# Re-ordering the preparation of a fused four-layer kernel: adapter tables laid out by the host, the convolution kernel's factors in another order, and its product behind two weight blocks

## The reference

```
x = x + mask * (causal_conv(mask*x, K) + D*mask*x)           # K[h,l] = 2 Re sum_n Cs[h,n] exp(dtA[h,n]*l), 64 states
x = x + einsum('bct,bcd->bdt', x, mix_weights[cond])          # 16 x 64 x 64
x = x + x @ base_weight.T + bias + (x @ A[ad].T) @ B[ad].T    # 32 adapters of rank 16
x = x + x @ W.T + 0.5 * (x @ lora_A[lab]) @ lora_B.T          # 5 labelers of rank 32
```

## Time and profile before

| | us |
|---|---|
| runs: median (lowest to highest) of 3 | 1478.62 (1477.57 to 1480.40) |
| the profiled execution, its own time | 1480.16 |
| its span in the profile | 1478.4 |
| preparation, to TensorE's first convolution matmul | 200.07 |
| convolution, to its last matmul | 571.4 |
| busy in the span: PE / VectorE / ScalarE / POOL | 1434.4 / 1140.7 / 612.5 / 119.0 |
| mean granted TensorE clock | 0.994 |

### The profile page before, as it was taken

How to read it: one execution, slowest core, us unless ns; L and a number is a source line. 1 busy time by engine, 2 the same in 40 slices (tenths; PEclk the granted TensorE clock), 3 DMA queues, 4 the chain that set the end, 5 groups by cost and what they waited for, 6 DMA issues and landing times.

```text
span 1478.4 us, 31603 instructions
## 1 busy us (share of the span) xinstructions
PE 1434.4 (97%) x9344; PEld 1330.9 (90%) x9344; DVE 1140.7 (77%) x2298; ACT 612.5 (41%) x1217; POOL 119.0 (8%) x188
## 2 busy tenths in 40 slices
PE   6989989999999997999999999999999999999998
PEld 5877879999999996889999999999999999999998
DVE  7974488888888885777777777777777777777775
ACT  3331256566666653334334334334334334334332
POOL 3460210000000000000000000000000000000000
PEclk9999999999999998999999999999999999999999
DMA  8034168888888887554655655655655655655652
GB/s 311 20 136 114 26 206 285 274 275 272 272 276 274 274 274 193 174 152 149 206 146 164 201 148 169 197 146 168 197 149 167 199 147 166 200 149 163 200 155 79
DMA packets 121523, 276.15 MB, mean 187 GB/s; under 512 B 23913, under 2 KB 64365, under 8 KB 118833
## 3 DMA queue, kind: packets, MB, share of 16 engines
q1 hardware_dynamic: 111308, 241.28, 54.1%
q10 hardware_dynamic: 10182, 34.46, 5.9%
HBM read 200.72 MB, written 74.95 MB: 186 GB/s over the span
## 4 chain that ended last, share of the span: by engine, by line
PE 86%; DVE 7%; DMA 3%; POOL 1%; issue 1%; ACT 1%; SPq 0%; DVEq 0%; ACTq 0%; POOLq 0%
PE ps L1601 18%; PE ps L1594 15%; PE ps L1232 13%; PE ps L1593 11%; PE ps L1574 8%; PE ps L1243 6%; PE ps L1134 4%; PE ps L1610 4%; PE ps L1223 3%; PE ps L1235 2%; DMA out<-y_out 1%; PE ps L1585 1%; DVE p L808 1%; DVE b3t L904 1%; DMA b_d<-b_last 1%
## 5 line engine op out<-in xcount | busy, mean ns | idle before, releaser
L1593 PE MATMUL ps<-weights,xa 128*128 128x256 f32 x1152 | 321.8, 282 | 2.3 <-ACT y_out L1384 1.6
L1594 PE MATMUL ps<-weights,xa 128*128 128x352 f32 x1152 | 322.7, 322 | 0.0
L1601 PE MATMUL ps<-weights,xs 128*128 128x512 f32 x1152 | 291.2, 401 | 0.0
L1601 PEld LDWEIGHTS ps<-weights,xs 128*128 128x128 f32 x1152 | 207.0, 189 | 40.4
L1232 PE MATMUL ps<-toep,ut 128*128 128x512 f32 (+2 forms) x1152 | 226.8, 342 | 0.0
L1593 PEld LDWEIGHTS ps<-weights,xa 128*128 128x128 f32 x1152 | 217.4, 189 | 4.9 <-issue 3.4
L1594 PEld LDWEIGHTS ps<-weights,xa 128*128 128x128 f32 x1152 | 216.2, 188 | 1.4
L1232 PEld LDWEIGHTS ps<-toep,ut 128*128 128x128 f32 x1152 | 194.3, 189 | 16.6
L1360 ACT ACTIVATE a<-ps 128x512 f32<-128x512 f32 x128 | 76.7, 599 | 288.1 <-PE ps L1574 272.6
L1574 PE MATMUL ps<-m_gath,x_in 128*128 128x128 f32 x1024 | 137.9, 279 | 10.3 <-DVE x_in L1459 10.3
L1574 PEld LDWEIGHTS ps<-m_gath,x_in 128*128 128x128 f32 x1024 | 129.6, 195 | 13.3 <-DVE x_in L1459 10.8
(11 more groups left out here) (223 smaller groups left out, 2262.6 us busy)
## 6 DMA issues: line engine op xcount, KB each, us to landing
lags<-kern_d SPq DMA_DIRECT2D x64, 512.0 KB, 5.0
xt<-in_xt SPq DMA_DIRECT2D x64, 512.0 KB, 5.7
x_d<-yo SPq DMA_DIRECT2D x64, 512.0 KB, 2.9
x_nat<-in_x SPq DMA_DIRECT2D x64, 512.0 KB, 3.8
x_in<-x_d SPq DMA_DIRECT2D x64, 512.0 KB, 5.6
out<-y_out ACTq DMA_DIRECT2D x62, 512.0 KB, 6.1
tab<-a_d SPq DMA_DIRECT2D x128, 128.0 KB, 2.1
stack<-b_d SPq DMA_DIRECT2D x126, 128.0 KB, 4.0
```

The costliest lines, as they stand in the source:

```text
L1593: mm(acc[:, left, 0:HALF], x_part, w[:, 0:HALF], start=start, stop=end, skip_group_check=True)
L1594: ins = mm(acc[:, right, 0:HALF + KR], x_part, w[:, HALF:WIDE], start=start, stop=end, skip_group_check=True)
L1601: ins = mm(acc[:, bank], operand[:, a, i, :], plain(i, b, m), start=opens and i == a == b == 0, stop=i == K4 - 1 and a == 1, skip_group_ch ...
```

## The change

The host lays out two inputs: the adapters' A as the table that a2_d was (so a2_d is the input itself), and the labelers' B transposed. Their transposes, copies, load and store go; the labelers' B is loaded straight into b3t after row has read it, and scaled there. The factors are formed with other instructions: POOL keeps the two first tables and the second table of turns, and VectorE does all products, the sum and the second decay table (twelve passes over 128x2048 on VectorE instead of ten, three on POOL instead of six). VectorE also makes the low part of b2_2. k0 and k1 come after d1 and d5. PSUM areas are dealt out anew; b2_3 is no longer in an area that the convolution uses. lower_low(0) moves ahead of six of the bias products, sums_low(0) and the halves of d1 and d5 ahead of the kernel's copy, and sums_low(3), which gets an argument that picks single subtractions, into channels 1 to 4. The mix load moves up on SP, behind the constants' stores; its additions on POOL come between the staging of d5 and the identities of d3 and d7. The late loads of d3 and d7 wait for `factors`. The lags of channel 1 get a buffer of their own, lags_first, which lies over yo0, so ScalarE waits before its first write to yo0.

```diff
     row_d = nc.dram_tensor("row_d", [2, T], F32).ap()
-    a2_d = nc.dram_tensor("a2_d", [A2N, P, K8 * R2], F32).ap()
...
-        ("c", 1), ("row", 0), ("b3", 3), ("k0", 2), ("k1", 1), ("la0", 0), ("la1", 3), ("la2", 2), ("la3", 1),
-        ("d1", 0), ("d5", 3), ("d2", 2), ("d6", 0), ("d3", 1), ("d7", 2), ("b2_3", 3)]
+        ("c", 1), ("row", 0), ("d1", 3), ("d5", 2), ("k0", 1), ("k1", 0),
+        ("d2", 3), ("d6", 2), ("d3", 1), ("d7", 2), ("b2_3", 0)]
     J = {name: j for j, (name, _) in enumerate(ORDER)}
...
+
+    def lags_of(k, u):
+
+        return lags_first if isinstance(k, int) and k == 0 and u == 1 else lags[u % BUFS]

...
             sp.dma_start(b2raw3[:], lora2_b[:, :, 3 * P:AR]).then_inc(in_b2_3, 16)
-            sp.dma_start(b3_raw[:], lora3_b).then_inc(in_b3, 16)

             sp.wait_ge(job_free, freed("a3b"))
             sp.dma_start(a3_d.rearrange("l p n -> p l n"), lora3_out[:].rearrange("p l c r -> p l (c r)")).then_inc(a3_stored, 16)
-            sp.wait_ge(job_done, done("a3b"))
-            sp.dma_start(lora_a_raw[:], lora2_a.rearrange("(c a) r t -> (a r) c t", c=AR // P)).then_inc(in_la, 16)
             for m in range(3):
                 sp.wait_ge(job_free, freed(f"b2_{m}"))
                 sp.dma_start(b2_rows[m * P:(m + 1) * P], f(b2_out[:])).then_inc(b2_stored, 16)
+            sp.wait_ge(job_done, done("row"))
...
             sp.dma_start(c_d[AR:AR + 1], c_row[:]).then_inc(c_stored, 16)
+            sp.wait_ge(factors, 1)
+            for v in range(2):
+                load_p2(p2_late[v], (3, 7)[v], in_late[v])
             sp.wait_ge(split_const, 4)
             sp.dma_start(row_d.unsqueeze(0), f(b2_out[0:1])).then_inc(const_stored, 16)
             sp.dma_start(b3_d, f(b2_out[B3_ROWS])).then_inc(const_stored, 16)
+            for half in range(2):
+                sp.dma_start(mix[C * half:C * half + C], mix_w.rearrange("s c d -> c s d")).then_inc(in_mix, 16)
             sp.wait_ge(kern_ready, 1)
             sp.dma_start(kern_d[:, 0:T].rearrange("h (q r) -> q h r", q=G), kern[:]).then_inc(kern_stored, 16)
-            sp.wait_ge(job_done, done("k1"))
-            for v in range(2):
-                load_p2(p2_late[v], (3, 7)[v], in_late[v])
-            sp.wait_ge(job_free, freed("la3"))
...
-            for half in range(2):
-                sp.dma_start(mix[C * half:C * half + C], mix_w.rearrange("s c d -> c s d")).then_inc(in_mix, 16)
             sp.wait_ge(p3_part, 1)
+            load_lags(0, 1)
             load_x(0, 1)
             sp.wait_ge(job_done, JOBS)
-            load_lags(0, 1)
             load_lags(0, 2)
...
             tt(fac_t[:], across(0), steps_of(0), ALU.mult).then_inc(fac_decay, 1)
-            pool.wait_ge(fac_exp, 1)
-            pool.wait_ge(fac_sin, 1)
-            link(tt(fac_u[:], fac_u[:], fac_t[:], ALU.mult))
-            tt(fac_u[:], fac_u[:], across(2), ALU.mult).then_inc(fac_sum, 1)
-            stage_low(4)
             pool.wait_ge(fac_arg, 2)
             tt(fac_v[:], across(1), steps_of(1), ALU.mult).then_inc(fac_turns, 1)
-            pool.wait_ge(fac_mid, 1)
-            tt(fac_t[:], across(0), steps_of(1), ALU.mult).then_inc(fac_decay, 1)
+            pool.wait_ge(staged_lo, 5)
             for n in range(5, len(STAGED)):
                 stage_low(n)
                 if n == 6:
+                    pool.wait_ge(in_mix, 32)
+                    for half in range(2):
+                        rows = slice(C * half, C * half + C)
+                        link(tt(mix[rows], mix[rows], ident[rows, C * half:C * half + C].unsqueeze(1).to_broadcast([C, S1, C]),
+                                ALU.add))
                     for v in range(2):
                         p2_identity(p2_late[v], (3, 7)[v], in_late[v])
-
-            pool.wait_ge(in_mix, 32)
-            for half in range(2):
-                rows = slice(C * half, C * half + C)
-                link(tt(mix[rows], mix[rows], ident[rows, C * half:C * half + C].unsqueeze(1).to_broadcast([C, S1, C]), ALU.add))
...
             act.wait_ge(part_ready, 1)
-            act.wait_ge(bias_ready, 1)
             lower_high(0)
             upper_high(0)
             act.wait_ge(fac_decay, 1)
             nc.scalar.activation(fac_t[:], fac_t[:], ACT.Exp).then_inc(fac_exp, 1)
+            stage_high(4)
             act.wait_ge(fac_arg, 1)
             trig(fac_u[:], -TWO_PI, phase[:, 3:4])
             act.wait_ge(fac_arg, 2)
             trig(fac_w[:], -TWO_PI, phase[:, 4:5])
             act.wait_ge(a3_stored, 16)
             b2_high(0, b2_out)
-            stage_high(4)
+            stage_high(5)
+            act.wait_ge(b2_stored, 16)
+            b2_high(1, b2_out)
             act.wait_ge(fac_decay, 2)
             nc.scalar.activation(fac_t[:], fac_t[:], ACT.Exp).then_inc(fac_exp, 1)
             act.wait_ge(fac_arg, 3)
             trig(fac_w[:], -TWO_PI, phase[:, 5:6])
-            for m in (1, 2):
-                act.wait_ge(job_done, done(f"b2_{m}"))
-                act.wait_ge(b2_stored, 16 * m)
-                b2_high(m, b2_out)
-                stage_high(m + 4)
+            act.wait_ge(b2_stored, 32)
+            b2_high(2, b2_out)
+            stage_high(6)

...
                 ready(act, x1_stored[u % 2], count_in(k, u, 2))
+                if isinstance(k, int) and k == u == 0:
+                    act.wait_ge(toep_lo, 2)
+                    act.wait_ge(tri_ready, 2)
                 copy(yo[u % 2][:, 0:HB], ps[2 + u % 2][:, 0:HB], ACT.Copy).then_inc(y_front, 1)
...

-            dve.wait_ge(w3_ready, K8)
-            bias_products(0, 2)
-            dve.wait_ge(job_done, done("par"))
-            t = target("par")
-            nc.vector.tensor_copy(part[:], t[:, HB:HB + 4 * C].rearrange("p (j h) -> p j h", j=4)).then_inc(part_ready, 1)
-            bias_products(2, K8)
...
                 tt(to[:, 1], target(f"b2_{m}"), f(to[:, 0]), ALU.subtract).then_inc(job_free, 1)

+            dve.wait_ge(w3_ready, K8)
+            bias_products(0, 2)
+            dve.wait_ge(job_done, done("par"))
+            t = target("par")
+            nc.vector.tensor_copy(part[:], t[:, HB:HB + 4 * C].rearrange("p (j h) -> p j h", j=4)).then_inc(part_ready, 1)
             dve.wait_ge(kern_stored, 16)
             lower_low(0)
+            bias_products(2, K8)
...
+                return grid[:, j, :].unsqueeze(1).to_broadcast([P, C, G])
+
+            dve.wait_ge(staged_hi, 5)
+            dve.wait_ge(staged_lo, 4)
+            tt(staged[0][:, 1], STAGED[4][1], f(staged[0][:, 0]), ALU.subtract).then_inc(staged_lo, 1)
...

+            dve.wait_ge(fac_sin, 1)
+            link(tt(fac_u[:], fac_u[:], across(2), ALU.mult))
+            dve.wait_ge(fac_sin, 2)
+            link(tt(fac_w[:], fac_w[:], across(3), ALU.mult))
+            b2_low(0, b2_out)
+            link(tt(fac_u[:], fac_u[:], fac_w[:], ALU.add))
             dve.wait_ge(fac_exp, 1)
-            dve.wait_ge(fac_sin, 2)
-            tt(fac_w[:], fac_w[:], fac_t[:], ALU.mult).then_inc(fac_mid, 1)
-            dve.wait_ge(fac_mid, 1)
-            link(tt(fac_w[:], fac_w[:], across(3), ALU.mult))
+            tt(fac_u[:], fac_u[:], fac_t[:], ALU.mult).then_inc(fac_sum, 1)
             dve.wait_ge(fac_sum, 1)
-            link(tt(fac_u[:], fac_u[:], fac_w[:], ALU.add))
-            b2_low(0, b2_out)
+            tt(fac_t[:], across(0), steps_of(1), ALU.mult).then_inc(fac_decay, 1)
             dve.wait_ge(fac_turns, 2)
             reduced(fac_w[:], fac_v[:], 2)
+            b2_low(1, b2_out)
             dve.wait_ge(fac_exp, 2)
             dve.wait_ge(fac_sin, 3)
             tt(fac_v[:], fac_w[:], fac_t[:], ALU.mult).then_inc(factors, 1)
-            b2_low(1, b2_out)
             b2_low(2, b2_out)
...
-            dve.wait_ge(job_done, done("b3"))
-            ts(b3t[B3_ROWS], target("b3")[0:R3, :], 0.5, None, ALU.mult).then_inc(job_free, 1)
-            dve.wait_ge(job_free, freed("b3"))
+            dve.wait_ge(in_b3, 16)
+            ts(b3t[B3_ROWS], b3t[B3_ROWS], 0.5, None, ALU.mult).then_inc(b3_scaled, 1)
+            dve.wait_ge(b3_scaled, 1)
+            dve.wait_ge(job_free, freed("row"))
             dve.wait_ge(b2_stored, 48)
...

+            sums_low(0)
+            dve.wait_ge(staged_lo, 7)
+            dve.wait_ge(c_stored, 32)
+            lower_low(1)
+            upper_low(1)
...
             tt(kern[:, :, G - 1], kern[:, :, G - 1], dcol[:], ALU.add).then_inc(kern_ready, 1)
-            for i in range(4):
-                dve.wait_ge(job_done, done(f"la{i}"))
-                nc.vector.tensor_copy(lora2_out[:, :, 2 * i:2 * i + 2, :].rearrange("p a c r -> p c a r"),
-                                      target(f"la{i}").rearrange("p (c a r) -> p c a r", c=2, a=A2N)).then_inc(job_free, 1)
-
-            dve.wait_ge(staged_lo, 7)
-            dve.wait_ge(c_stored, 32)
-            lower_low(1)
-            upper_low(1)
-            sums_low(0)
             sums_low(1)
             dve.wait_ge(staged_lo, 9)
```

(28 more changed lines are left out.)

39 lines of the change are left out of this document (19 added, 20 removed).

## The result

| | before | after |
|---|---|---|
| median of the comparison's runs (4 each) | 1479.07 | 1456.82 |
| ratio | | 0.9847 [0.9835, 0.9858] |
| the profiled execution, own time / span | 1480.16 / 1478.4 | 1456.56 / 1454.8 |
| first matmul of b2_0 / c / b2_3 | 56.6 / 95.8 / 186.5 | 52.8 / 85.6 / 168.2 |
| first matmul of convolution 0 / 3 | 200.1 / 220.2 | 179.0 / 198.1 |

The change saves 22.3 us. I had forecast 18.2 and a time of 1460.4: the direction was right, the size 4 us short, and the time lies at the lower edge of the range given. 22.1 us of it are there when convolution 3 begins (220.2-198.1), and nothing is lost in the long stages behind it. The two profiled executions are 23.6 us apart; 1.2 of the rest lies at the passage from the convolution to the products, which varies from execution to execution.

A forecast was written before the change was run, and what follows sets the result against it. TensorE, busy 97% of the span, was taken as the bound, so only removed matmuls and stops could gain. 1.6+6.3+1.0+7.3+2.5-0.5 = 18.2 us off the median 1478.62 gave 1460.4 us, range 1456.8 to 1465.2.

The forecast's parts named there:

- step 1: Ahead of b2_0: d0's low half moves before six bias products, so b2_0 no longer waits; gain 1.6 us.
- step 2: Ahead of b2_2: its low half moves to VectorE, removing the 4.76 us wait and 1.52 of slow clock; gain 6.3 us.
- step 8: End of preparation: mix's additions and VectorE's last four sums leave, removing the wait before convolution 0; gain 2.5 us.
- step 9: Before convolution 3: last store taken as 7.0 us, wait 2.8 us where it was 2.3; gives back 0.5 us.
- Steps 3 and 4: Between c and d1: b3's eight transposes go, gain 1.0 us, and the lora_A jobs go, gain 7.3 us.
- Step 5: k moves behind d1 and d5: factors ready near 97, k asked for at 122.6; cost nothing.
- Step 6: Ahead of d2: mix's load, additions and identities move before POOL's staging of d2; cost 0 to 0.4, taken as 0.
- C: At d2: it waits behind mix on POOL, the constants' split being no earlier; saving 12 to 16, about 1464.6; chance 0.10.
- D: Same place as C, mix landing after 136 us: slower than before, 1481 or more; chance 0.02.
- E: At b2_2: still waits because VectorE's low half comes after 81; 6.3 us missing, 1466.7; chance 0.03.
- rival B: Channel 3 eats nothing: store takes 5.2 us; saving 20.0 to 21.0, 1458.6 to 1457.6; chance 0.12.
- rival A: Channel 3 eats more: store takes 8.06 us and the clock falls; saving 15.6, 1463.0; chance 0.20.

The follow-up runs named there:

- again: Each kernel run a second time without edit: before 1480.45 us, changed 1459.07 us (ratio 0.9854 to the kernel before).
- third: Each kernel run a third time without edit: before 1481.13 us, changed 1457.51 us (ratio 0.9844 to the kernel before).
- bias_first: Changed kernel with the six bias products ahead of d0's low half again: 1461.26 us, ratio 0.9875 to the kernel before.
- low_half_pool: Changed kernel with b2_2's low half back on POOL, behind its tables: 1462.95 us, ratio 0.9880 to the kernel before.
- Old_factors: Changed kernel with the factors' products and the order of b2_low(1) and b2_high(1) as before: 1466.08 us, ratio 0.9911 to the kernel before.
- the tables alone: Kernel before with only both host layouts and without jobs b3 and la0 to la3: 1468.90 us, ratio 0.9920 to the kernel before.
- k_early: Changed kernel with k0, k1 and VectorE's copy of them ahead of d1 and d5 again: 1457.74 us, ratio 0.9852 to the kernel before.
- sums_back: Changed kernel with sums_low(3) whole in front of the convolution again: 1457.55 us, ratio 0.9850 to the kernel before.
- mix_late: Changed kernel with the mix load and its additions where they were before: 1458.74 us, ratio 0.9856 to the kernel before.
- no_last_store: Changed kernel without b2_last's store and channel 3's wait for it, adapters 24 to 31 wrong: 1456.64 us, ratio 0.9833 to the kernel before.

## Why the prediction came out short

The three executions of each kernel (the first profile, again, third) give each stage's mean; the table sets it against the steps' sums.

| stage | before | after | gain | forecast |
|---|---|---|---|---|
| to b2_0 (step 1) | 56.0 | 53.3 | 2.7 | 1.6 |
| b2_0 to c (step 2) | 38.8 | 32.8 | 6.0 | 6.3 |
| c to b2_3 (steps 3 to 6) | 92.2 | 82.6 | 9.6 | 8.3 |
| b2_3 to convolution 0 (step 8) | 13.5 | 10.9 | 2.6 | 2.5 |
| convolution 0 to 3 (step 9) | 20.3 | 19.1 | 1.2 | -0.5 |
| sum | 220.8 | 198.7 | 22.1 | 18.2 |

- **Step 1** had the right mechanism (bias_first puts the stop back) and was mis-sized by 1.1. I read 1.58 us off an execution in which TensorE was late by its own chance. b2_0's start before was set by VectorE (55.7 to 56.6 in three executions), while TensorE was there at 53.2 and 53.6 in the other two. In the changed kernel TensorE keeps its early arrival.
- **Step 2** gave nearly the right number for the changed kernel and the wrong owner. TensorE has no stop ahead of b2_2, and the stage is 6.0 us shorter. That this is so near 6.3 is in part luck: the 4.76 us that I took was the longest of three stops (3.22 and 3.14 in the others), and in those two executions 1.6 us of slow clock behind b2_0's stop, which no term of mine held, filled the gap. And "VectorE does it" is worth -2.0 us alone and -2.5 us beside the tables, since the gain then ends in the wait for b2_low(2). It pays in the changed kernel (low_half_pool, which undoes it, takes 6 us more), where the factors are ready at 96 and b2_low(1) goes ahead of the last product. The prediction costed the factors at nothing for want of a wait at k, and did not ask what would be late next between b2_2 and k. Old_factors puts their new order at about 8 us; the parts overlap, so the prices of the parts do not add up.
- **Steps 3 and 4** had the right mechanism and were mis-sized by 1.3: 8.3 us forecast, 9.6 measured, and the tables alone gave 9.5 at convolution 3. From c to b2_3 the three executions of before took 90.7, 92.7 and 93.2: in the first one the adapter jobs' stops kept the clock, in the others a stop of 2.88 or 4.57 us was followed by a granted clock of 0.50 and 0.59, and the matmuls from there to b2_3 were busy 2.7 and 1.5 us longer (70.49 and 69.28 us for 67.82). I had priced the one execution.
- **Step 5**: factors at 95.9, k at 120.3 (forecast 97 and 122.6). That k moves is worth nothing was right, and k_early shows it.
- **Step 6**: no cost, as taken. Rivals C, D and E did not occur: mix landed at 114.0, d2's low half had 2.4 us to spare.
- **Step 8** was right in size; sums_back and mix_late show that one of its two reasons would have done. What counts is steps 8 and 9 together, since in both kernels the start of convolution 3 hangs on one chain: VectorE's last low half, its store, the x load. From b2_3's first matmul to convolution 3 it takes 33.7, 33.8 and 33.9 us before and 29.9, 29.8 and 30.2 after: 3.8 less, where the two steps had 2.0.
- **Step 9** is the step that failed: "7.0, and that I take" for the last store, which made the forecast 1.6 us too small. It measured 5.43, 5.24 and 5.62 us in the changed kernel, and 8.06 to 8.3 in the kernel before, so that the stop ahead of convolution 3 is 1.65, 1.48 and 1.88 us and not 2.8. (It is no shorter than before on the mean, where it was 2.31, 1.15 and 1.47 us; the chain as a whole is shorter.) This is rival B, to which I gave 0.12 because I worked out a rate from one crowded stretch. The lags of channel 1 had already landed when the store began. A slip of 0.2 us is in the same step: three periods of 5.75 and 0.3 from 181.4 give 199.0, not 199.2.
- **The clock** kept 1.00 through the last stop in every execution of the changed kernel, so the 1.5 us of rival A did not come. That is in part luck, since bias_first lost its clock there behind 1.85 us. The nearest row to 2.8 us in the first profile was not the 2.31 us stop that I used but the 2.52 us ahead of convolution 0, and it kept the clock too.
- **The range**: C's middle is 1464.6, and the upper end of 1465.2 does not follow from it. The measured 1456.82 lies at the other end, where B's 1457.6 less the spread was.

So in the changed kernel the waits went and stayed where the prediction had them, and three terms were too small: step 1 by 1.1 us, steps 3 and 4 by 1.3, step 9 with its store by 1.6. Two of the three came from reading one execution, the third from a rate of one crowded stretch.

What stays open: of the gain of 22.3, the ratio's interval alone is 3.4 us wide. From the convolution's last matmul to the first matmul with the combined weight it takes 13.9, 15.1 and 17.2 us before and 16.0, 17.0 and 18.5 in the changed kernel (14.3 to 16.3 in its variants), by a cause not looked into. That the shorter store is due to fewer loads ahead of it is argued: no run changes the loads alone. No version was clearly faster than the changed kernel: k_early equals it, and no_last_store, which leaves values out, is 1.7 us ahead at convolution 3.

## What to carry to other kernels

Price a stop from several executions, as the time at which the releaser is done less the time at which the waiting engine would arrive, and look for the slack of the next such release (here 0.4 to 2.0 us ahead of k, seen only as the end of one VectorE instruction beside the start of a TensorE row). A gain that passes one wait is only as large as the slack at the next, so a set of edits has to clear the whole chain, and each alone may even cost time. Where a serial program removes all its stops of 2 us and more, add what the clock took behind them to the forecast.
